# VectorE writes the low part of x from the PSUM bank in the first four groups of the first FFN

## Chip, core and metric

The kernel runs on one core of a Trainium2 chip. The metric is the device time of one launch in microseconds (us); lower is better. Engines are TensorE (PE in the profile), VectorE (DVE), ScalarE (ACT), GpSimd (POOL) and SyncE (SP), each with an instruction stream of its own that runs in order; they are kept in step by semaphores.

## What is computed

x has 32 sequences of 256 tokens with 128 features. The block is a macaron: half an FFN, attention, half an FFN, each on a layernorm of x and added to x.

```python
x = x + 0.5 * ffn(layernorm(x), router_w, w1, w2)
x = x + attn(layernorm(x), W_qkv, W_out)      # 16 heads of 8, rotary, elu+1 features, linear attention
x = x + 0.5 * ffn(layernorm(x), router_w, w1, w2)
...
probs = sigmoid(x @ router_w.T)               # 8 experts, widths 4 x 128 and 4 x 256
topw, sel = top_k(probs, 2); topw = topw / topw.sum()
h = square(relu(x @ W1[e])); y = h @ W2[e]; out = sum over e of y * combine[e]
```

The kernel computes all experts for all tokens and scales the hidden units by the square root of the routing weight before they are squared.

## The kernel before

A **group** is two sequences, 512 tokens; there are 16 (NG). Three streams run over the groups, one behind the other: `f1` (first FFN), `at` (attention) and `f2` (second FFN, SHIFT = 5 groups behind f1). Every engine runs the same loop of rounds t = -3 to 21, and the order in a round is written out by hand in its `iteration(t, par)`. In round t, f1's group t + 2 is transposed, scored by the router and has its weights broadcast; group t + 1 is in its up and down products; group t + 3 gets its layernorm statistics.

A round has 24 places (1536 hidden units are 12 chunks of 128). As long as f2 has not begun, f1 is alone (`alone`) and its 12 chunks take every second place; afterwards f1 has places 0 to 11 and f2 12 to 23.

Matmuls in fp32 precision are built from three products of high and low parts: `x_hi`, the value rounded to fp32r, and `x_lo`, what is left. The path of a group of f1 at its start:

1. `norm` (ACT, L697) writes xn; `transpose` (PE, L471) puts xn's transpose into the bank `tp`.
2. `evacuate_x` (ACT, L709) copies `tp` to `xT` in SBUF.
3. `logits` (PE, L490) multiplies xT by the router and writes the result **into tp**, over the transpose.
4. `exp_logits` (ACT, L718 ex, L722 odds), `take_sigmoid` (DVE, L972 prob), `best_two` to `choose_two` (DVE), `root_of_weights` (POOL, L874), `spread_roots` (DVE, L1025, L1031), `weight_rows` (PE, L480), `rows_of_weights` (ACT, L730), and in `broadcast` (SP) two DMAs: to DRAM (L395) and back over all partitions into `g_all` (L407, four pieces).
5. `high_part` (DVE, L965) casts xT to `x_hi` and raises s_hi; `low_part` (POOL, L868) subtracts it from xT into `x_lo` and raises s_lo. The first up product of the group waits for s_lo.
6. Per chunk: `up` (PE, L509 to L511), `weighted` (DVE, L1047, hid; the first of a group waits for the first piece of g_all), `squares` (ACT, L740 the square, L751 h_hi), `remainders` (POOL, L880, h_lo), `down` (PE, L529 to L531).

The order around the change: DVE has weighted(t, 0), then high_part of f1's group t + 2, then weighted(t, 1). PE has places 0 to 2, then logits of group t + 2, then the filler transposes `keep_busy` (L589: 36 in round -2, 16 in round -1) and place 3 on; chunk 2 is at place 4 and waits for the hid of chunk 0. ACT has exp_logits of group t + 2 ahead of the squares of places 0 to 2. POOL has low_part of group t + 2, then the h_lo of places 0 and 1, then `inv_std` (L856 ve, L857, L859 rstd, L861 nbias) of group t + 3, which waits for `mean_variance` (DVE, L957); that one stands behind place 4 and take_sigmoid. `norm` of group t + 3 waits for nbias.

```python
if c < 2:
    m = turns(s, t) * NC
    ...
m = n * NC + max(c - 1, 0)
if due(m):
    pe.wait_ge(s_z[s], value(m))
```

Of the kernel before, what the change touches and what calls it, by code (L numbers as in the profile page):

```python
# [27 lines left out]
F32 = mybir.dt.float32  # L28
F32R = mybir.dt.float32r
ALU = mybir.AluOpType  # L30
# [33 lines left out]
SHIFT = 5  # L64
T_FIRST, T_LAST = -3, NG + SHIFT

class Step:
# [14 lines left out]
    @property  # L82
    def last(self):
        return self.c + self.a * (self.trips - 1)

    @property
    def value(self):
        return self.i * self.a + self.c


def first(v):
    return v.c if isinstance(v, Step) else v
# [16 lines left out]
def live(n):  # L109

    return first(n) >= 0 and last(n) < NG


def first_time(stream, n):

    return stream and not isinstance(n, Step) and n == 0
# [51 lines left out]
def build(nc, x_in, wqkv, wout, router, w1, w2, const, out, rows):  # L168
    ctx = ExitStack()
    with ctx:  # L170
        def sb(name, shape, dt=F32):
            return ctx.enter_context(nc.sbuf_tensor(name, shape, dt))
# [35 lines left out]
        x_hi = {s: [sb(f"x_hi_{s}{u}", [P, NTOK], F32R) for u in range(nx[s])] for s in STREAMS}  # L208
        x_lo = {s: [sb(f"x_lo_{s}{u}", [P, NTOK], F32R) for u in range(nx[s])] for s in STREAMS}
# [53 lines left out]
        tp = bank[0]  # L263
# [16 lines left out]
        def per(name, keys):  # L280
            return {s: sem(f"s_{name}_{s}") for s in keys}
# [9 lines left out]
        s_hi = per("hi", STREAMS)  # L291
        s_lo = per("lo", STREAMS)
# [37 lines left out]
        def alone(s, t):  # L330


            return not live(t + 1 - SHIFT) if s == "f1" else not live(t + 2)

        def lonely(s, n):

            return n < SHIFT if s == "f1" else n >= NG - 1 - SHIFT

        def aside(s, n):

            return lonely(s, n) and ((SHIFT - n) % 2 == 1 if s == "f1" else (NG - SHIFT - n) % 2 == 0)
# [105 lines left out]
        def _(pe):  # L447
# [35 lines left out]
            def logits(s, n):  # L483
                if not live(n):
                    return
                pe.wait_ge(s_xT[s], value(n + 1))
                if first_time(s == "f1", n):
                    pe.wait_ge(s_router, 16)
                for k in range(TG):
                    i = mm(tp[:, k * P:k * P + PAD], xT[s][:, k * P:(k + 1) * P], router_sb[:], start=True, stop=True)  # L490
                i.then_inc(s_logit[s], 1)
# [150 lines left out]
            def iteration(t, par):  # L642
                transpose("f1", t + 2, t, 0)
                quarter(t, 0, par)
                state(t - 2)
                logits("f1", t + 2)
                if first_time(True, t + 2):
                    keep_busy(a2, 36)
# [15 lines left out]
                out_proj(t - 2)  # L664
                q(t - 1)
                logits("f2", t + 2 - SHIFT)
                quarter(t, 5, par)
                weight_rows("f1", t + 2, t, 4)
# [171 lines left out]
        def _(pool):  # L840
# [20 lines left out]
                gp.tensor_tensor(nbias[s][:], nm[s][:], rstd[s][:], ALU.mult).then_inc(s_nb[s], 1)  # L861

            def low_part(s, n, par):
                if not live(n):
                    return
                u = par if nx[s] == 2 else 0
                pool.wait_ge(s_hi[s], value(n + 1))
                gp.tensor_tensor(x_lo[s][u][:], xT[s][:], x_hi[s][u][:].bitcast(F32), ALU.subtract).then_inc(s_lo[s], 1)  # L868
# [14 lines left out]
            def iteration(t, par):  # L883
                remainders(t - 1, 21, 22)
                low_part("f1", t + 2, par)
                remainders(t - 1, 23)
                remainders(t, 0, 1)
                inv_std("f1", t + 3)
                remainders(t, 2, 3, 4, 5, 6)
                root_of_weights("f1", t + 2)  # L890
                remainders(t, 7)
                low_part("at", t - 1, 0)
                remainders(t, 8, 9, 10)
                low_part("f2", t + 2 - SHIFT, (par + SHIFT) % 2)
                remainders(t, 11)
                remainders(t, 12, 13, 14, 15)
                inv_std("at", t)
                remainders(t, 16, 17, 18)
                root_of_weights("f2", t + 2 - SHIFT)
                remainders(t, 19)  # L900
                inv_std("f2", t + 3 - SHIFT)
                remainders(t, 20)
                if first_time(True, t + 2):
                    pool.wait_ge(s_w2hi, 1)
                    gp.tensor_tensor(w2_lo[:], w2_raw.rearrange("p (c d) -> p c d", c=NC),
                                     w2_hi[:].bitcast(F32), ALU.subtract).then_inc(s_w2lo, 1)
# [5 lines left out]
        def _(dve):  # L912
            v = nc.vector
# [46 lines left out]
            def high_part(s, n, par):  # L960
                if not live(n):
                    return
                u = par if nx[s] == 2 else 0
                dve.wait_ge(s_xT[s], value(n + 1))
                v.tensor_copy(x_hi[s][u][:], xT[s][:]).then_inc(s_hi[s], 1)  # L965


            def take_sigmoid(s, n):
# [183 lines left out]
            def iteration(t, par):  # L1152
# [7 lines left out]
                q_features(t - 2)  # L1160
                weighted(t, 0)
                high_part("f1", n1, par)
                spread_roots("f2", n2_last, 0)
                weighted(t, 1)
# [23 lines left out]
                normalise(t - 2, 2)  # L1188
                weighted(t, 10)
                high_part("at", t - 1, 0)  # L1190
                choose_two("f1", n1)
                weighted(t, 11)
                weighted(t, 12)
                high_part("f2", n2, p2)
                spread_roots("f1", n1, 0)
                weighted(t, 13)
# [63 lines left out]
```

## Time and profile before

| what | us |
|---|---|
| median of 3 runs (lowest, highest) | 792.01 (791.9, 795.37) |
| the profiled execution | 793.06 |
| its span, first to last instruction | 791.3 |
| GpSimd busy in the span | 686.2 (87%) |
| TensorE busy | 729.2 (92%) |
| VectorE, ScalarE busy | 581.6 (74%), 597.5 (76%) |
| mean granted clock of TensorE | 0.993 |

The page gives, for each engine, its busy time, then its busy share in 40 slices, the chain of work that ended last, and the costliest groups of instructions. The timelines list single instructions with their start, their duration and, in brackets, how long the engine had been idle and who released it. The matmuls of one engine overlap, so their starts say more than their durations. A busy share is a mean over the span: the first 100 us, where the pipeline of groups fills, have other limits than the rest.

### The profile page before, as it was taken

To read this page: it belongs to the slowest core of one execution; us is meant where nothing else is said; L and a number is where in the kernel's file an instruction comes from. 1 tells how busy PE (TensorE), PEld (TensorE's weight loads), DVE (VectorE), ACT (ScalarE), POOL (GpSimd) and SP (SyncE) were. 2 spreads that over 40 slices of the span, in tenths; PEclk is the share of its full clock that TensorE was granted. 3 is DMA by queue.
4 is the path that set the end of the run, shared out by engine and by line. 5 is a ranking of instruction groups with operands and counts; after the bars stand their busy time and mean duration, and the time that the engine had idled before them with its cause. 6 is when DMAs were issued, how large, how long until landed. Compare 5 with 4: busy or idle time off the path is not lost.

```text
span 791.3 us, 13302 instructions
## 1 busy us (share of the span) xinstructions
PE 729.2 (92%) x3736; PEld 594.3 (75%) x3736; DVE 581.6 (74%) x1832; ACT 597.5 (76%) x1220; POOL 686.2 (87%) x668
## 2 busy tenths in 40 slices
PE   6688788889999999999999999999999998989887
PEld 6466566667888888888888888888887877767665
DVE  3456788877879787877878797878777678676543
ACT  4577677668887978888888879788878766766765
POOL 3778867859999999999999999999999877666876
PEclk9999999989999999999999999999999999999999
DMA  5654113023233222233333332213333403303330
GB/s 181 187 163 133 37 72 107 2 107 108 108 109 121 91 91 69 99 110 108 121 109 120 109 122 84 79 68 112 116 108 121 122 2 107 110 13 121 121 121 27
DMA packets 31160, 79.38 MB, mean 100 GB/s; under 512 B 3312, under 2 KB 14448, under 8 KB 31088
## 3 DMA queue, kind: packets, MB, share of 16 engines
q1 hardware_dynamic: 30800, 78.47, 29.9%
q8 instruction: 30, 0.49, 0.3%
q14 instruction: 42, 0.34, 0.1%
q10 hardware_dynamic: 288, 0.07, 0.0%
HBM read 73.81 MB, written 4.72 MB: 99 GB/s over the span
## 4 chain that ended last, share of the span: by engine, by line
PE 27%; DVE 27%; POOL 18%; issue 13%; ACT 10%; DMA 4%; DVEq 1%; POOLq 0%; ACTq 0%; SPq 0%
POOL h_lo L880 9%; DVE hid L1047 7%; POOL root_f L874 4%; PE bank L509 4%; PE bank L529 3%; PE bank L511 3%; PE bank L510 3%; PE bank L531 3%; PE bank L530 3%; DMA g_all_f<-rows_f 3%; ACT h_hi L751 3%; DVE pick_f L1025 2%; ACT hid L740 2%; POOL x_lo_at L868 2%; ACT xn_f L697 2%
## 5 line engine op out<-in xcount | busy, mean ns | idle before, releaser
L880 POOL TENSOR_TENSOR h_lo<-hid,h_hi 128x512 fp32r<-128x512 f32 x384 | 492.8, 1308 | 70.0 <-ACT h_hi L751 69.4
L1047 DVE SCALAR_TENSOR_TENSOR hid<-bank,g_all_f 128x512 f32<-128x512 f32 x384 | 262.2, 684 | 137.8 <-PE bank L511 90.9
L740 ACT ACTIVATE hid<-hid 128x512 f32<-128x512 f32 x384 | 228.8, 622 | 50.0 <-DVE hid L1047 49.7
L751 ACT ACTIVATE h_hi<-hid 128x512 fp32r<-128x512 f32 x384 | 225.8, 620 | 4.9 <-PE bank L531 0.4
L509 PE MATMUL bank<-x_hi_f,w_hi 128*128 128x512 f32 x384 | 164.3, 428 | 16.1 <-DVE hid L1047 16.1
L529 PE MATMUL bank<-h_hi,w_hi 128*128 128x512 f32 x384 | 154.5, 402 | 12.5 <-POOL h_lo L880 12.5
L531 PE MATMUL bank<-h_hi,w_lo 128*128 128x512 f32 x384 | 152.6, 397 | 0.0
L511 PE MATMUL bank<-x_hi_f,w_lo 128*128 128x512 f32 x384 | 151.9, 396 | 0.0
L530 PE MATMUL bank<-h_lo,w_hi 128*128 128x512 f32 x384 | 151.9, 396 | 0.0
L510 PE MATMUL bank<-x_lo_f,w_hi 128*128 128x512 f32 x384 | 151.5, 395 | 0.0
L509 PEld LDWEIGHTS bank<-x_hi_f,w_hi 128*128 128x128 f32 x384 | 73.1, 190 | 40.7 <-DVE hid L1047 25.2
L529 PEld LDWEIGHTS bank<-h_hi,w_hi 128*128 128x128 f32 x384 | 72.5, 189 | 34.9 <-POOL h_lo L880 20.0
L511 PEld LDWEIGHTS bank<-x_hi_f,w_lo 128*128 128x128 f32 x384 | 72.6, 189 | 17.6
L531 PEld LDWEIGHTS bank<-h_hi,w_lo 128*128 128x128 f32 x384 | 72.4, 188 | 16.6
L530 PEld LDWEIGHTS bank<-h_lo,w_hi 128*128 128x128 f32 x384 | 72.5, 189 | 15.4
L510 PEld LDWEIGHTS bank<-x_lo_f,w_hi 128*128 128x128 f32 x384 | 73.3, 191 | 11.1
L697 ACT ACTIVATE xn_f<-x_sb,nbias_f,rstd_f 128x128 f32<-128x128 f32 x128 | 52.4, 481 | 12.5 <-POOL nbias_f L861 12.5
L874 POOL TENSOR_TENSOR root_f<-cwt_f,c_half 128x8 f32<-128x8 f32 x32 | 54.3, 1697 | 0.0
L868 POOL TENSOR_TENSOR x_lo_f<-xT,x_hi_f 128x512 fp32r<-128x512 f32 x32 | 41.5, 1298 | 12.9 <-DVE x_hi_f L965 12.9
L709 ACT ACTIVATE xT<-bank 128x512 f32<-128x512 f32 x48 | 28.3, 590 | 26.4 <-PE bank L471 16.7
L965 DVE CAST x_hi_f<-xT 128x512 fp32r<-128x512 f32 x32 | 21.6, 676 | 24.3 <-ACT xT L709 24.3
L718 ACT ACTIVATE ex_f<-bank 128x32 f32<-128x32 f32 x32 | 6.3, 197 | 43.0 <-PE bank L490 43.0
(105 smaller groups left out, 1045.2 us busy)
## 6 DMA issues: line engine op xcount, KB each, us to landing
g_all_f<-rows_f SPq DMA_DIRECT2D x128, 512.0 KB, 5.8
x_sb<-in_x SPq DMA_DIRECT2D x16, 256.0 KB, 3.3
out_x<-x_sb SPq DMA_DIRECT2D x16, 256.0 KB, 7.1
g_all_f<-in_w SPq DMA_DIRECT2D x2, 768.0 KB, 6.6
con<-in_const SPq DMA_DIRECT2D x1, 584.0 KB, 6.1
rows_f<-g_row_f SPq DMA_DIRECT2D x32, 16.0 KB, 1.4
g_all_f<-in_wqkv SPq DMA_DIRECT2D x1, 192.0 KB, 6.5
con<-in_const ACTq DMA_DIRECT2D x1, 68.0 KB, 3.2
```

Of the source, the lines that this page charges most:

```text
L509: mm(o, w1_hi[:, w], x_hi[s][u][:], start=True, stop=False)
L510: mm(o, w1_hi[:, w], x_lo[s][u][:], start=False, stop=False)
L511: mm(o, w1_lo[:, w], x_hi[s][u][:], start=False, stop=True).then_inc(s_p1[s], 1)
L529: mm(o, w2_hi[:, c, :], h_hi[:, c, :], start=(c == 0), stop=False)
L530: mm(o, w2_hi[:, c, :], h_lo[:, c, :], start=False, stop=False)
L531: i = mm(o, w2_lo[:, c, :], h_hi[:, c, :], start=False, stop=(c == NC - 1))
L697: i = fn(xn[s][:, k, :], tile, ACT.Identity, bias=nbias[s][:, k:k + 1], scale=rstd[s][:, k:k + 1])
L740: fn(h, h, ACT.Square).then_inc(s_sq[s], 1)
L751: fn(h_hi[:, c, :], hid[:, c % STAGE, :], ACT.Copy).then_inc(s_hhi[s], 1)
L874: gp.tensor_tensor(root[s][:], cwt[s][:], c_half[:], ALU.pow).then_inc(s_root[s], 1)
L880: gp.tensor_tensor(h_lo[:, c, :], hid[:, c % STAGE, :], h_hi[:, c, :].bitcast(F32), ALU.subtract).then_inc(s_hlo[s], 1)
L1047: v.scalar_tensor_tensor(hid[:, c % STAGE, :], hp[c % 2][:], 0.0, g_all[s][:, EXPERT[c], :], ALU.max, ALU.mult).then_inc(s_z[s], 1)
```

## The change

For f1's groups 0 to 3 (`low_from_bank`), VectorE does the subtraction itself, right behind the cast: it waits for its own s_hi, reads the transpose from the bank `tp` and not from the copy xT, writes x_lo and raises s_lo. GpSimd's low_part returns at once for these groups. Since the logits overwrite `tp`, TensorE's logits of these groups wait for s_lo as well. Lines behind the first edit move down by 4 to 10.

```diff
--- before.py
+++ after.py
@@ -332,6 +332,10 @@
 
             return not live(t + 1 - SHIFT) if s == "f1" else not live(t + 2)
 
+        def low_from_bank(s, n):
+
+            return s == "f1" and n < SHIFT - 1
+
         def lonely(s, n):
 
             return n < SHIFT if s == "f1" else n >= NG - 1 - SHIFT
@@ -484,6 +488,8 @@
                 if not live(n):
                     return
                 pe.wait_ge(s_xT[s], value(n + 1))
+                if low_from_bank(s, n):
+                    pe.wait_ge(s_lo[s], value(n + 1))
                 if first_time(s == "f1", n):
                     pe.wait_ge(s_router, 16)
                 for k in range(TG):
@@ -861,7 +867,7 @@
                 gp.tensor_tensor(nbias[s][:], nm[s][:], rstd[s][:], ALU.mult).then_inc(s_nb[s], 1)
 
             def low_part(s, n, par):
-                if not live(n):
+                if not live(n) or low_from_bank(s, n):
                     return
                 u = par if nx[s] == 2 else 0
                 pool.wait_ge(s_hi[s], value(n + 1))
@@ -963,6 +969,10 @@
                 u = par if nx[s] == 2 else 0
                 dve.wait_ge(s_xT[s], value(n + 1))
                 v.tensor_copy(x_hi[s][u][:], xT[s][:]).then_inc(s_hi[s], 1)
+                if low_from_bank(s, n):
+                    dve.wait_ge(s_hi[s], value(n + 1))
+                    v.tensor_tensor(x_lo[s][u][:], tp[:], x_hi[s][u][:].bitcast(F32), ALU.subtract) \
+                        .then_inc(s_lo[s], 1)
 
 
             def take_sigmoid(s, n):
```

VectorE's order from the end of the set-up into round -2; f1's x tiles are named x_hi_f and x_lo_f, w_lo is the low part of w1. Before:

```order
L922 TENSOR_TENSOR w_lo<-g_all_f,w_hi 128x1536 [waits s_w1hi]
L965 CAST x_hi_f<-xT 128x512 [waits s_xT_f1]
L948 BN_STATS bn_f<-x_sb 128x6 [waits s_load1,s_nb_f1]
L948 BN_STATS bn_f<-x_sb 128x6 x3
L972 RECIPROCAL prob_f<-odds_f 128x32 [waits s_odds_f1]
```

After:

```order
L928 TENSOR_TENSOR w_lo<-g_all_f,w_hi 128x1536 [waits s_w1hi]
L971 CAST x_hi_f<-xT 128x512 [waits s_xT_f1]
L974 TENSOR_TENSOR x_lo_f<-bank,x_hi_f 128x512 [waits s_hi_f1]
L954 BN_STATS bn_f<-x_sb 128x6 [waits s_load1,s_nb_f1]
L954 BN_STATS bn_f<-x_sb 128x6 x3
L982 RECIPROCAL prob_f<-odds_f 128x32 [waits s_odds_f1]
```

A subtraction with the bank as its operand stands between the cast and the statistics; in each of the next three rounds it stands likewise behind the cast, which follows the first hid product:

```order
L1057 SCALAR_TENSOR_TENSOR hid<-bank,g_all_f 128x512 [waits s_p1_f1,s_ga_f10]
L971 CAST x_hi_f<-xT 128x512 [waits s_xT_f1]
L974 TENSOR_TENSOR x_lo_f<-bank,x_hi_f 128x512 [waits s_hi_f1]
L1057 SCALAR_TENSOR_TENSOR hid<-bank,g_all_f 128x512 [waits s_p1_f1]
L954 BN_STATS bn_f<-x_sb 128x6 [waits s_load0,s_nb_f1]
L954 BN_STATS bn_f<-x_sb 128x6 x3
L1057 SCALAR_TENSOR_TENSOR hid<-bank,g_all_f 128x512 [waits s_p1_f1,s_ga_f11]
```

VectorE before, at the same place in round -1:

```order
L1047 SCALAR_TENSOR_TENSOR hid<-bank,g_all_f 128x512 [waits s_p1_f1,s_ga_f10]
L965 CAST x_hi_f<-xT 128x512 [waits s_xT_f1]
L1047 SCALAR_TENSOR_TENSOR hid<-bank,g_all_f 128x512 [waits s_p1_f1]
L948 BN_STATS bn_f<-x_sb 128x6 [waits s_load0,s_nb_f1]
L948 BN_STATS bn_f<-x_sb 128x6 x3
L1047 SCALAR_TENSOR_TENSOR hid<-bank,g_all_f 128x512 [waits s_p1_f1,s_ga_f11]
```

The new row is behind the hid product that waits for the broadcast (s_ga_f10), and before the hid product of chunk 1.

TensorE in round -1, from the up product of chunk 1 over the logits and the fillers to chunk 2, before:

```order
L509 MATMUL bank<-x_hi_f,w_hi 128x512
L510 MATMUL bank<-x_lo_f,w_hi 128x512
L511 MATMUL bank<-x_hi_f,w_lo 128x512
L490 MATMUL bank<-router_sb,xT 128x96 [waits s_xT_f1]
L490 MATMUL bank<-router_sb,xT 128x96 x3
L589 MATMUL bank<-con 128x128 x16
L509 MATMUL bank<-x_hi_f,w_hi 128x512 [waits s_z_f1]
L510 MATMUL bank<-x_lo_f,w_hi 128x512
L511 MATMUL bank<-x_hi_f,w_lo 128x512
```

After:

```order
L515 MATMUL bank<-x_hi_f,w_hi 128x512
L516 MATMUL bank<-x_lo_f,w_hi 128x512
L517 MATMUL bank<-x_hi_f,w_lo 128x512
L496 MATMUL bank<-router_sb,xT 128x96 [waits s_lo_f1,s_xT_f1]
L496 MATMUL bank<-router_sb,xT 128x96 x3
L595 MATMUL bank<-con 128x128 x16
L515 MATMUL bank<-x_hi_f,w_hi 128x512 [waits s_z_f1]
L516 MATMUL bank<-x_lo_f,w_hi 128x512
L517 MATMUL bank<-x_hi_f,w_lo 128x512
```

The order is the same; the logits have s_lo_f1 as a further wait, which VectorE now raises behind its first hid product.

GpSimd's order loses the x_lo rows of groups 0 to 3 and nothing takes their place: the one of group 0 stood ahead of inv_std of group 1, the others each ahead of the h_lo of place 0 of their round.

## Rows read from the trace of the kernel before

**Rows 1.** Busy tenths of GpSimd in 40 equal slices of the span, from the page

```profile
POOL 3778867859999999999999999999999877666876
```

**Rows 2.** Waits, 0 to 170 us: waiting instruction, releaser, us in total, times, longest

```profile
DVE hid L1047 <- DMA g_all_f<-rows_f: 15.6, 3, 7.1
```

**Rows 3.** Timeline, round -2: start us, us, engine, line, instruction [idle before]

```profile
11.27 1.13 PE L490 MATMUL bank<-router_sb,xT 128*128 128x96 f32 x8 [0.69 <-ACT xT L709]
...
12.33 0.42 DVE L965 CAST x_hi_f<-xT 128x512 fp32r<-128x512 f32 x1
...
12.66 0.32 ACT L722 ACTIVATE odds_f<-ex_f,c_one 128x32 f32<-128x32 f32 x1
...
13.45 0.33 DVE L972 RECIPROCAL prob_f<-odds_f 128x32 f32<-128x32 f32 x1
...
15.81 1.63 POOL L874 TENSOR_TENSOR root_f<-cwt_f,c_half 128x8 f32<-128x8 f32 x1
```

**Rows 4.** Timeline, round -1, same columns

```profile
20.69 1.04 PE L490 MATMUL bank<-router_sb,xT 128*128 128x96 f32 x8
...
21.56 1.91 PE L589 MATMUL bank<-con 128*128 128x128 f32 x16
...
26.05 0.69 DVE L1047 SCALAR_TENSOR_TENSOR hid<-bank,g_all_f 128x512 f32<-128x512 f32 x1 [7.11 <-DMA g_all_f<-rows_f]
26.66 0.42 DVE L965 CAST x_hi_f<-xT 128x512 fp32r<-128x512 f32 x1
...
26.80 0.51 PE L509 MATMUL bank<-x_hi_f,w_hi 128*128 128x512 f32 x1 [3.33 <-DVE hid L1047]
...
27.71 0.64 ACT L740 ACTIVATE hid<-hid 128x512 f32<-128x512 f32 x1 [0.30 <-DVE hid L1047]
...
28.37 0.67 DVE L1047 SCALAR_TENSOR_TENSOR hid<-bank,g_all_f 128x512 f32<-128x512 f32 x1
28.94 1.29 POOL L880 TENSOR_TENSOR h_lo<-hid,h_hi 128x512 fp32r<-128x512 f32 x1 [0.49 <-ACT h_hi L751]
...
29.22 0.32 DVE L957 BATCH_NORM_AGGREGATE mv_f<-bn_f 128x2 f32<-128x6 f32 x4
...
30.19 0.20 POOL L856 TENSOR_TENSOR ve_f<-mv_f,c_eps 128x4 f32<-128x4 f32 x1
...
30.61 1.01 POOL L859 TENSOR_TENSOR rstd_f<-ve_f,c_mhalf 128x4 f32<-128x4 f32 x1
```

**Rows 5.** Timeline, round 0

```profile
47.67 1.03 PE L490 MATMUL bank<-router_sb,xT 128*128 128x96 f32 x8
...
49.47 0.69 DVE L1047 SCALAR_TENSOR_TENSOR hid<-bank,g_all_f 128x512 f32<-128x512 f32 x1 [4.12 <-DMA g_all_f<-rows_f]
...
52.36 1.30 POOL L880 TENSOR_TENSOR h_lo<-hid,h_hi 128x512 fp32r<-128x512 f32 x1 [0.48 <-ACT h_hi L751]
```

**Rows 6.** Timeline, round 1

```profile
72.45 1.02 PE L490 MATMUL bank<-router_sb,xT 128*128 128x96 f32 x8
...
73.64 0.69 DVE L1047 SCALAR_TENSOR_TENSOR hid<-bank,g_all_f 128x512 f32<-128x512 f32 x1 [4.38 <-DMA g_all_f<-rows_f]
...
74.25 0.66 DVE L965 CAST x_hi_f<-xT 128x512 fp32r<-128x512 f32 x1
...
76.78 1.31 POOL L880 TENSOR_TENSOR h_lo<-hid,h_hi 128x512 fp32r<-128x512 f32 x1 [0.49 <-ACT h_hi L751]
```

**Rows 7.** Groups of VectorE over the span: count | busy us, mean ns | idle before

```profile
L1055 DVE TENSOR_TENSOR x_sb<-bank,x_sb 128x512 f32<-128x512 f32 x32 | 21.7, 680 | 6.4 <-PE bank L542 6.4
```

**Rows 8.** TensorE's timeline, then busy us by stretch; granted clock third from last

```profile
88.20 0.50 PE L556 MATMUL bank<-x_hi_at,wq_hi 128*128 128x512 f32 x1 [3.47 <-POOL x_lo_at L868]
...
168.55 0.80 PE L509 MATMUL bank<-x_hi_f,w_hi 128*128 128x512 f32 x1 [2.47 <-DVE hid L1047]
...
170.00:172.00 2.00, 2.00 (x11) 2.00 (x10) 0.69 (x1) 0.00 (x0) 0.44 (x1) 0.51 0.00 0
172.00:174.00 2.00, 2.00 (x14) 1.79 (x14) 0.31 (x1) 1.01 (x4) 0.00 (x0) 1.00 0.00 0
```


## The prediction

> **What bounds the kernel now.** I read the slices of the page first. GpSimd (the page's POOL) shows 8 tenths or less in most of the first nine slices and nines only from there on [rows 1]: it bounds the steady part, not the start. The change touches groups 0 to 3 of the first FFN alone, so the question is what bounds the first 80 us. There the waits say that VectorE (DVE) stood 15.6 us in three waits for the broadcast of the routing weights [rows 2]: nobody is full, and each round is one serial loop. Its members, in the timelines: logits, ScalarE (ACT) ex and odds, VectorE's top two, GpSimd's root, the g_row copy, the two DMAs, the first hid product, its square and high part, GpSimd's first h_lo, rstd of a later group, and so on. A microsecond put on this loop has no idle time behind it that would take it back. I call the rounds t = -2 to 1; round t transposes and scores group t + 2.
>
> **What the change does to the order.** VectorE gets one instruction per round, right behind the x_hi cast. GpSimd loses one. The third edit matters most: TensorE's logits, which overwrite the bank that VectorE now reads, must also wait for x_lo. In rounds -1, 0 and 1 the x_hi cast stands behind the first hid product in VectorE's order, and that one waits for the broadcast. Today the logits are long done by then: in round -1 they start at 20.69, and x_hi only at 26.66 [rows 4]; in round 0 at 47.67 against a first hid at 49.47 [rows 5]; in round 1 at 72.45 against 73.64 [rows 6]. Afterwards they start behind hid, x_hi and x_lo. Queued behind them are, on TensorE, the filler transposes of round -1 and the up product of chunk 2, and on ScalarE ex and odds, which stand ahead of the square of chunk 0.
>
> **Price of the new subtraction.** No row has it as such. Nearest is x_sb<-bank,x_sb, a two-operand operation on 128x512 with one operand in the bank: 680 ns over 32 of them [rows 7]. The hid product, also from a bank, takes 0.69 [rows 4]. From below, the cast alone takes 0.42 and from above GpSimd's own 1.3 bounds it. I take 0.69; the lower end would take 4 x 0.27 = 1.1 us from the sum below, the upper end add 4 x 0.61 = 2.4. Waiting on the engine's own last result costs little: the cast of 12.33 ends at 12.75, and I allow 0.03 for the wait.
>
> **Round -2.** Now logits start at 11.27, x_hi at 12.33 for 0.42, odds at 12.66 for 0.32, prob at 13.45 (held back by the statistics in front of it, since odds ended at 12.98), root at 15.81 [rows 3]. Afterwards x_lo runs 12.78 to 13.47, logits start at 13.53 (+2.26), odds end at 15.24, prob starts at 15.30: **+1.85** for all that follows, root among it. GpSimd's saved 1.27 doesn't shorten this, since its next work waits for VectorE.
>
> **Round -1.** From the first hid at 26.05: x_hi 26.66 to 27.08, x_lo 27.11 to 27.80, logits at 27.86. Two branches then meet in rstd (GpSimd L859, now at 30.61) [rows 4].
> - ScalarE: from the start of the logits to the start of odds it is 1.39 (11.27 to 12.66 [rows 3]), 0.23 more to the square of chunk 0, 0.54 to that of chunk 1: 30.0. Today the latter is at 27.71 and h_lo 1.23 later, at 28.94. So h_lo would come at 31.3, +2.35.
> - TensorE: the logits take 0.96 before the next can start, 16 filler transposes 1.87 (1.91 with the last one's tail), so the up product of chunk 2 starts at 30.7 instead of 26.80. It takes 0.9, hid of chunk 2 starts at 31.6 instead of 28.37. From that start to the end of mean and variance (29.22 plus 0.32) is 1.17 today: 32.8, and rstd 0.5 later at 33.3 (ve starts 0.42 before rstd, at 30.19), **+2.7**. This one is last.
>
> **Rounds 0 and 1.** There are no fillers, only one down product (0.7) between logits and chunk 2. Round 0: hid 49.47, x_hi at 50.08, x_lo until 51.22, logits 51.28 instead of 47.67; odds 52.7, squares 52.9 and 53.5, h_lo 54.7 instead of 52.36 [rows 5]: **+2.4**. The TensorE branch gives a mean and variance at 55.7, before that h_lo ends at 56.0, so it is covered by 0.3. Round 1: x_hi takes 0.66 there [rows 6], x_lo ends at 75.63, h_lo 79.1 instead of 76.78: **+2.4**. GpSimd's three low parts of 1.3 us in these rounds lie in idle time today (it waits for h_hi behind each), so leaving them out gives nothing. VectorE's extra work of 0.69 is inside these sums.
>
> At full clock the sum is 1.85 + 2.7 + 2.4 + 2.4 = 9.35 us.
>
> **The clock.** In round -1 TensorE would stand from the end of chunk 1's up product (the logits followed it at 20.69) until 27.86, 7 us, where today the gap is 3.33 [rows 4]. The longest gap of the first 100 us, 3.47 us before 88.20, left the granted clock at 1.00; but one of 2.47 us before 168.55 is followed by a granted clock of 0.51 in the stretch 170 to 172, half speed being 1.2 of 2.4 GHz, and by 1.00 from 172; the L509 matmul that ends that gap takes 0.80 [rows 8], the one that ends the gap of 3.33 takes 0.51 [rows 4]. A gap twice the longest that was borne will, I think, cost the clock. From 168.55 to 172 the clock was low for some 3.4 us. At up to twice their time the logits (0.96) take about 1.8 and the first half of the fillers (0.93) about 1.6, which uses those 3.4 us up; the other half takes 0.93 as before: 4.3 instead of 2.8, **+1.5**. Rounds 0 and 1 have gaps of 3.6 and 3.2, like the two that kept the clock; I leave them at full speed, with up to 0.8 for the logits and 1 for the chunk-2 branch each if they don't.
> The Trainium skill, page "TensorE: Matmul & The Clock Gate", Part 1, has the rule behind this: idleness throttles the array to half clock, and activity releases it. By that rule alone each of the three rounds is at risk, and the sum could be 13; by the two gaps of rows 4 and 8 only the longest is. The same page, Part 4 (PE-mode transpose), says that transposes don't count as activity, so that the fillers would not bring the clock back; no row here decides that for fillers alone after a fall, and by it round -1 would cost about 1 us more.
>
> **Sum: 9.35 + 1.5 = 10.85 us.** The profiled execution took 793.06 (span 791.3 and 1.8 around it), 1.05 above the median of 792.01. Put on the profiled execution the sum gives 803.9, on the median 802.9. I forecast the median's.
>
> **Rivals.**
> - *Full clock everywhere*: 792.0 + 9.35 = 801.3. For it: two gaps over 3 us did no harm. Against: 7 us is another length.
> - *Half clock in two or more rounds*: 1 to 1.8 us more for each of rounds -2, 0, 1: 804 to 807. For it: the fall after 2.47 us.
> - *Part of the delay is given back*: if later rounds have slack, for example because loads of x that share the DMA engines are over by then and the broadcasts land sooner, it might be up to half: 792 + 5.4 = 797.4. Against: VectorE stood idle for the broadcasts themselves [rows 2], and no row shows other work that the start waits for.
> - *The logits' wait doesn't bind* and only the instruction put into VectorE's order counts: 4 x 0.7 = 2.8 us, 795. That needs x_lo to come before the logits would start anyway; the orders and rows 4 to 6 speak against it in three of four rounds.
> - *Faster*: GpSimd, the engine that bounds the steady part, loses 4 x 1.30 = 5.2 us: 787. It decides if GpSimd's queue, not ScalarE's h_hi, were last before each first h_lo in rounds -1 to 1. It would have to stand without a wait there, and in each of them it begins h_lo after waiting. The four low parts lie outside the slices where GpSimd is full [rows 1].
>
> **Chances.** Forecast 0.40; full clock 0.22; more half clock 0.20; part given back 0.09; insertion only 0.05; faster 0.04. The range is 798.5 to 806.5: it leaves out the last two, some of the highest, and half of the given-back case, less than 2 in 10. 0.5% (4.0 us) is about what a measurement of this kernel can tell from no change. Slower by more than that: the first four, 0.91 less a little, 0.90; within: 0.06; faster: 0.04.
>
> **What the profile after would show.** The subtraction from the bank at about 0.69; logits of rounds -1, 0 and 1 starting 1.8 to 2.1 us behind the start of the first hid, with TensorE released by VectorE's x_lo; square of chunk 0 behind odds; rstd +2.7 to +4 late in round -1; the first hid late by 1.9 in round -1, 6.1 in round 0, 8.5 in round 1 and 10.9 in round 2 (at about 96 us today), and constant from there; a granted clock under 1 near 30 us. Wrong would be: a broadcast that lands on time although g_row is late, a shift at 100 us that is not there at the end, or logits that start as early as today.

## The result and the profile after

The changed kernel takes 805.42 us in the median of 6 runs, the kernel before 791.95 of 6 on the same chip: a ratio of 1.0171, 95% interval 1.0152 to 1.019. It is slower by 13.5 us; the forecast was 10.9 slower, at 802.9, with a range of 798.5 to 806.5. The profiled execution of the changed kernel took 804.79 (span 803.0).

The page of the changed kernel: busy time by engine, granted clock of TensorE in 40 slices, and two costly groups (busy us, mean ns | idle before, releaser).

```profile
PE 734.1 (91%) x3736; PEld 600.2 (75%) x3736; DVE 584.6 (73%) x1836; ACT 597.2 (74%) x1220; POOL 681.2 (85%) x664
...
PEclk9899899999999999999999999999999999999999
...
L724 ACT ACTIVATE ex_f<-bank 128x32 f32<-128x32 f32 x32 | 6.3, 198 | 60.0 <-PE bank L496 60.0
L496 PE MATMUL bank<-router_sb,xT 128*128 128x96 f32 x256 | 36.6, 291 | 14.9 <-DVE x_lo_f L974 12.3
```

GpSimd is 5 us less busy and VectorE 3 us more, as the diff says. But TensorE now stands idle 14.9 us ahead of the logits (0.7 before), 12.3 of it for VectorE's x_lo, and ScalarE's ex waits 60.0 us for the logits (43.0 before). The clock row has two eights, in the slices that hold rounds -1 and 1. The waits of 0 to 110 us name the steps behind that (us in total, times, longest); GpSimd's wait for the first of these was 11.6 us before:

```profile
POOL h_lo L886 <- ACT h_hi L757: 25.2, 8, 7.2
ACT ex_f L724 <- PE bank L496: 21.7, 4, 7.9
...
PE bank L496 <- DVE x_lo_f L974: 12.3, 3, 5.6
```

Now the timeline, in the same columns as [rows 3 to 6]. Round -2 of the changed kernel:

```profile
13.69 1.10 PE L496 MATMUL bank<-router_sb,xT 128*128 128x96 f32 x8 [2.67 <-issue]
...
17.79 1.63 POOL L880 TENSOR_TENSOR root_f<-cwt_f,c_half 128x8 f32<-128x8 f32 x1
...
20.76 0.34 SPq L399 DMA_DIRECT2D rows_f<-g_row_f  x1
22.24 0.81 SPq L411 DMA_DIRECT2D g_all_f<-rows_f  x2
```

Root comes 1.98 later than in [rows 3]. Round -1:

```profile
26.53 0.69 DVE L1057 SCALAR_TENSOR_TENSOR hid<-bank,g_all_f 128x512 f32<-128x512 f32 x1 [5.60 <-DMA g_all_f<-rows_f]
...
27.59 0.69 DVE L974 TENSOR_TENSOR x_lo_f<-bank,x_hi_f 128x512 fp32r<-128x512 f32 x1
...
28.43 2.00 PE L496 MATMUL bank<-router_sb,xT 128*128 128x96 f32 x8 [5.59 <-DVE x_lo_f L974]
30.21 3.28 PE L595 MATMUL bank<-con 128*128 128x128 f32 x16
...
32.70 1.29 POOL L886 TENSOR_TENSOR h_lo<-hid,h_hi 128x512 fp32r<-128x512 f32 x1 [7.15 <-ACT h_hi L757]
33.25 0.48 PE L515 MATMUL bank<-x_hi_f,w_hi 128*128 128x512 f32 x1
...
35.98 1.01 POOL L865 TENSOR_TENSOR rstd_f<-ve_f,c_mhalf 128x4 f32<-128x4 f32 x1
```

The logits started ahead of the first hid product in [rows 4], at 20.69; now they start behind it and behind both halves of x, and take 2.00 instead of 1.04. The fillers take 3.28 instead of 1.91, so that the up product of chunk 2 starts 4.8 us behind the start of the logits. From the first hid to rstd it is 9.45 us where [rows 4] have 4.56. Rounds 0 and 1 have the same order, again with slow logits:

```profile
54.85 0.69 DVE L1057 SCALAR_TENSOR_TENSOR hid<-bank,g_all_f 128x512 f32<-128x512 f32 x1 [4.13 <-DMA g_all_f<-rows_f]
...
56.74 1.86 PE L496 MATMUL bank<-router_sb,xT 128*128 128x96 f32 x8 [3.54 <-DVE x_lo_f L974]
...
62.88 1.01 POOL L865 TENSOR_TENSOR rstd_f<-ve_f,c_mhalf 128x4 f32<-128x4 f32 x1
...
82.42 0.69 DVE L1057 SCALAR_TENSOR_TENSOR hid<-bank,g_all_f 128x512 f32<-128x512 f32 x1 [4.33 <-DMA g_all_f<-rows_f]
...
84.61 2.00 PE L496 MATMUL bank<-router_sb,xT 128*128 128x96 f32 x8 [3.15 <-DVE x_lo_f L974]
...
91.04 1.01 POOL L865 TENSOR_TENSOR rstd_f<-ve_f,c_mhalf 128x4 f32<-128x4 f32 x1
```

TensorE by stretch (columns: length, busy us with instructions, granted clock, DMA share, GB/s):

```profile
28.00:30.00 2.00, 1.57 (x7) 0.50 1.00 386
30.00:32.00 2.00, 2.00 (x11) 0.50 0.64 220
32.00:34.00 2.00, 2.00 (x12) 0.75 0.48 164
...
58.00:60.00 2.00, 2.00 (x7) 0.50 0.72 249
...
86.00:88.00 2.00, 2.00 (x7) 0.50 0.01 4
```

0.50 is 1.2 of 2.4 GHz. The prediction had the clock low in round -1 alone; it was low in all three. Each time the engine had stood still for the wait just before. In shorter stretches the low clock lasts from 26.2 to 33.0 us in round -1, from 56.9 in round 0 and from 84.2 in round 1.

### The profile page after: what moved, and what is told of

Read it like the earlier page. It is cut to its first block, busy times and chain, and to the rows that moved or that the text cites. A ratio compares the mean times of both kernels' runs of the same rounds, so it can differ in the third digit from the quotient of the medians.

```text
span 803.0 us, 13305 instructions
## 1 busy us (share of the span) xinstructions
PE 734.1 (91%) x3736; PEld 600.2 (75%) x3736; DVE 584.6 (73%) x1836; ACT 597.2 (74%) x1220; POOL 681.2 (85%) x664
## 4 chain that ended last, share of the span: by engine, by line
PE 30%; DVE 28%; issue 14%; POOL 12%; ACT 11%; DMA 4%; DVEq 1%; POOLq 0%; ACTq 0%; SPq 0%
DVE hid L1057 8%; POOL h_lo L886 5%; POOL root_f L880 4%; PE bank L515 4%; PE bank L517 3%; PE bank L535 3%; PE bank L516 3%; PE bank L537 3%; PE bank L536 3%; DMA g_all_f<-rows_f 3%; PE bank L496 3%; ACT h_hi L757 3%; DVE pick_f L1035 2%; ACT hid L746 2%; POOL x_lo_at L874 2%
## 5 line engine op out<-in xcount | busy, mean ns | idle before, releaser
L535 PE MATMUL bank<-h_hi,w_hi 128*128 128x512 f32 x384 | 155.2, 404 | 10.4 <-POOL h_lo L886 10.4
L517 PEld LDWEIGHTS bank<-x_hi_f,w_lo 128*128 128x128 f32 x384 | 72.9, 190 | 17.6
L703 ACT ACTIVATE xn_f<-x_sb,nbias_f,rstd_f 128x128 f32<-128x128 f32 x128 | 52.5, 481 | 11.3 <-POOL nbias_f L867 11.3
L496 PE MATMUL bank<-router_sb,xT 128*128 128x96 f32 x256 | 36.6, 291 | 14.9 <-DVE x_lo_f L974 12.3
L496 PEld LDWEIGHTS bank<-router_sb,xT 128*128 128x128 f32 x256 | 35.3, 208 | 17.8 <-issue 16.4
```

What stands on the lines that cost most here:

```text
L517: mm(o, w1_lo[:, w], x_hi[s][u][:], start=False, stop=True).then_inc(s_p1[s], 1)
L535: mm(o, w2_hi[:, c, :], h_hi[:, c, :], start=(c == 0), stop=False)
```

## The experiments

Where a round is named, "hid to rstd" is the time from the start of its first hid product to the start of rstd in that round. In the profiled kernel before it is 4.56, 4.58 and 4.83 in rounds -1, 0 and 1; in the changed kernel 9.45, 8.03 and 8.62. The difference given for a run is that of its median to the median of the kernel before on the same chip.

### Which part costs: the wait, the instruction, or the bank

**Only the wait.** This is the kernel before, with GpSimd still subtracting; TensorE's logits of groups 0 to 3 wait for x_lo:

```
@@ logits(s, n), kernel before
+                if s == "f1" and n < SHIFT - 1:
+                    pe.wait_ge(s_lo[s], value(n + 1))
```

> The kernel before, with one edit: TensorE's logits of groups 0 to 3 also wait for s_lo, which GpSimd raises as before. Theory W (the stall of the logits is the cost): x_lo comes from GpSimd some 0.2 us later than from VectorE (1.29 instead of 0.69 long, but the first work after the cast), so 805 to 807. Theory I (the instruction put into VectorE's order is the cost): no VectorE instruction is added, so 792. The square of chunk 1 may come 0.6 us earlier than in the changed kernel, but it stands behind odds, so that should not show.

809.39 against 793.03 us, ratio 1.0197 (1.0165 to 1.0228), 16.4 us slower, and above the 805 to 807 that was expected. The wait in its trace:

```profile
PE bank L492 <- POOL x_lo_f L870: 13.6, 3, 5.8
```

Hid to rstd is 10.56 in round -1 and 8.65 in round 0. The wait alone costs more than the change. GpSimd's subtraction takes 1.27 where VectorE's takes 0.69, and from the start of the cast to the logits it is 1.91 in round -1 where the changed kernel has 1.29: the logits come 0.6 later a round. The clock was low in round -2 as well, which it wasn't in the profiled changed kernel. How the 2.9 us between the two runs divide between these isn't settled.

**Only the instruction.** VectorE subtracts from xT in SBUF, so the logits need no new wait:

```
@@ VectorE, kernel before (GpSimd leaves these groups out, as in the change)
+                if low_from_bank(s, n):
+                    dve.wait_ge(s_hi[s], value(n + 1))
+                    v.tensor_tensor(x_lo[s][u][:], xT[s][:], x_hi[s][u][:].bitcast(F32), ALU.subtract) \
+                        .then_inc(s_lo[s], 1)
```

> The changed kernel without the logits' wait for s_lo; since the bank may then be overwritten, VectorE subtracts from xT in SBUF and not from the bank. Theory W: no stall, so only hid of chunk 1 comes 0.7 us later in rounds -1, 0 and 1, which shifts the square of chunk 1, h_hi and the first h_lo: 792 + 3 x 0.7 = 794, with round -2 absorbed. Theory I: the whole 13 us stays, 805.

794.41 against 793.03 us, ratio 1.0018 (1.0001 to 1.0035), 1.4 us slower. Hid to rstd is 5.29, 5.29 and 5.95: the 0.7 of the instruction each time, and about 1.1 in round 1.

**The same change, logits into another bank.** VectorE still reads the bank; only the shared bank is gone, and with it the logits' wait (the next transposes into the first bank wait for x_lo instead):

```
@@ logits(s, n) and ex, changed kernel; the fillers go to a1
-                if low_from_bank(s, n):
-                    pe.wait_ge(s_lo[s], value(n + 1))
...
-                    i = mm(tp[:, k * P:k * P + PAD], xT[s][:, k * P:(k + 1) * P], router_sb[:], start=True, stop=True)
+                    i = mm((a2 if low_from_bank(s, n) else tp)[:, k * P:k * P + PAD], xT[s][:, k * P:(k + 1) * P], router_sb[:], start=True, stop=True)
```

> The changed kernel, but the logits of groups 0 to 3 go into another bank that is free then (the fillers go to a third), so they need not wait for x_lo; VectorE still reads the transposed x from its bank and writes the low part. The wait for x_lo moves to the next writer of that bank. Theory (the shared bank's wait is what costs): logits start as early as before, in rounds -1 to 1 ahead of the first hid product, rstd minus first hid at 5.3, 5.3 and 5.9 as where VectorE subtracted without the wait; 793 to 795. Rival (reading the bank on VectorE is itself the cost): 800 or more.

794.94 against 791.97 us, ratio 1.0044 (1.0029 to 1.0059), 3.0 us slower. Its round -1:

```profile
23.13 1.85 PE L496 MATMUL bank<-router_sb,xT 128*128 128x96 f32 x8
...
25.40 0.69 DVE L1057 SCALAR_TENSOR_TENSOR hid<-bank,g_all_f 128x512 f32<-128x512 f32 x1 [5.71 <-DMA g_all_f<-rows_f]
...
30.70 1.01 POOL L865 TENSOR_TENSOR rstd_f<-ve_f,c_mhalf 128x4 f32<-128x4 f32 x1
```

The logits run ahead of hid again and hid to rstd is 5.30. (They take 1.85 because the clock was low from 18.5 to 25.3 us in this execution, behind a gap of 2.44 us; the first hid waits for the DMA anyway.) With the bank shared the change costs 13.5, with the logits elsewhere 3.0: the wait for the shared bank is shown to be the cause of some 10.5 us. The 3.0 that are left (2.3 to 4.7) fit the price of the rival "insertion only" (2.8); the run with only the instruction measured 1.4 (0.1 to 2.8).

### Which groups cost

The test in low_from_bank is narrowed to one group:

```
@@ low_from_bank(s, n), changed kernel
-            return s == "f1" and n < SHIFT - 1
+            return s == "f1" and n == 0
```

> The change for group 0 alone. In the trace of the changed kernel g_row is written 1.98 us late in round -2, but the first hid starts only 0.48 us late, since the first rows DMA took 1.5 instead of 3.2 us. Theory of the give-back by that DMA: 792.4, no difference to be measured. Theory of the prediction's sum: +1.85, 793.8. In the trace the rows DMA of round -2 is to land near 22.2 us.

Group 0 alone (round -2): 794.05 against 793.03 us, ratio 1.0012 (0.9997 to 1.0028). Its DMA of the routing rows is issued at 20.91, 2.1 later than in the kernel before, but only 1.0 of it stands in the time. The interval, -0.2 to 2.2 us, takes in no change and the forecast 1.85 alike, so the run doesn't decide between them. This trace also showed a thing that the change doesn't cause: that DMA took 3.44 us, where the changed kernel's had taken 1.48.

With `n == 1` in place of `n == 0`:

> The change for group 1 alone. Theory W with the clock: round -1 costs 4.9 us as in the trace of the changed kernel (stall of 5 to 6 us, logits and fillers at half clock), 797, and rounds 0 and 1 are as before. Theory W without the clock: 2.7 us, 794.7. If the delay of one round is given back later, under 794.

Group 1 alone (round -1): 796.41 against 793.03 us, ratio 1.0039 (1.0022 to 1.0055), 3.4 us slower. In its trace the logits wait and run slowly in round -1 alone:

```profile
24.66 0.69 DVE L1057 SCALAR_TENSOR_TENSOR hid<-bank,g_all_f 128x512 f32<-128x512 f32 x1 [5.10 <-DMA g_all_f<-rows_f]
...
26.56 1.99 PE L496 MATMUL bank<-router_sb,xT 128*128 128x96 f32 x8 [3.59 <-DVE x_lo_f L974]
...
34.96 1.01 POOL L865 TENSOR_TENSOR rstd_f<-ve_f,c_mhalf 128x4 f32<-128x4 f32 x1
```

Hid to rstd is 10.3 here, 5.7 above the kernel before, of which 3.4 reach the end (1.7 to 4.4). The DMAs of the routing rows say where most of the rest went: against the second execution of the kernel before (below) the one at 162 us is 6.6 later and the one at 186 only 5.0, which then stays until 765 us; the spans differ by 4.5. In between, the clock is low in both traces, at different places (158 to 161 and 168 to 171 us in that one, 163 to 169 in this one); whether that is the cause isn't shown.

### What the clock costs

**Fillers ahead of the wait in rounds -1 to 1.** They keep TensorE busy while it waits. No work is left out:

```
@@ TensorE's iteration(t, par), changed kernel
                 state(t - 2)
+                if not isinstance(t, Step) and -1 <= t <= 1:
+                    keep_busy(a2, 40 if t == -1 else 24)
                 logits("f1", t + 2)
```

> The changed kernel with filler transposes ahead of the logits, where TensorE stands: 40 in round -1, 24 each in rounds 0 and 1, at 0.11 us each, so that they end before x_lo is there. Theory C (half clock is worth about 4 us in rounds -1 to 1): granted clock stays at 1.00 until 90 us, first hid of rounds 0, 1 and 2 come 1.4, 2.6 and 4 us earlier than in the changed kernel, 801. If the stall alone costs and the clock does not: 805.

805.13 against 792.45 us (ratio 1.0136, 1.01 to 1.0173); one of its four runs took 799.29. In the profiled execution hid to rstd is 7.24, 7.26 and 7.26, that is 2.7, 2.7 and 2.4 above before; round 0 was still partly slow, behind a gap of 2.47 us that the 24 fillers left. So the steps from hid to rstd went as the full-clock sum says, but the time hardly moved: 805 was the number expected if the clock were worth nothing. The trace shows two other delays. Round -2 had no fillers ahead of its logits, so they ran at half clock behind a gap of 3.62 us (1.96 us long, where the changed kernel has 1.10), and the DMA of the rows was issued 0.8 late, at 21.58. And in round 0 SyncE took 4.28 us to issue the four pieces of g_all, where the changed kernel and the next run take 1.78, and the first hid came 7.22 us behind the issue of the rows instead of 5.50; nothing in the edit explains that one. Together they are 2.5 us, and the span is 2.4 longer than that of the next run (803.1 against 800.7). Round -2 shows one thing more:

```profile
15.41 4.93 PE L595 MATMUL bank<-con 128*128 128x128 f32 x36
```

```profile
14.00:16.00 2.00, 2.00 (x11) 0.50 0.00 0
...
18.00:20.00 2.00, 2.00 (x21) 1.00 0.00 0
```

From 15.41 to 20.3 TensorE runs nothing but the 36 fillers that stand behind the logits of round -2 (here the busy time is TensorE's alone), and in the midst of them, at 17.1, the clock comes back.

**Fillers in all four rounds, and more of them:**

```
+                if -2 <= t <= 1:
+                    keep_busy(a2, (20, 40, 36, 26)[t + 2])
```

> The changed kernel, with filler transposes ahead of the logits' wait in all four rounds: 20, 40, 36 and 26 of them, to keep TensorE busy up to x_lo. The work is whole otherwise. Theory (sum of full-clock terms 9.35, less 0.5 to 1 that comes back at the end): granted clock 1.00 through 10 to 90 us, rstd minus first hid +2.7, +2.4, +2.4 against before, the first out_x some 9.3 later, 799.5 to 801.5. Rival (the clock falls elsewhere whatever is filled, or fillers delay what stands behind them): 803 to 806.

801.32 against 791.97 us, ratio 1.0115 (1.0099 to 1.0131), 9.35 us slower (7.8 to 10.4), which is the full-clock sum of the prediction. That it agrees to the digit is partly chance, as the rows DMAs below show. Round -1 in its trace, then TensorE by stretch:

```profile
26.44 0.69 DVE L1059 SCALAR_TENSOR_TENSOR hid<-bank,g_all_f 128x512 f32<-128x512 f32 x1 [5.58 <-DMA g_all_f<-rows_f]
...
28.55 1.03 PE L496 MATMUL bank<-router_sb,xT 128*128 128x96 f32 x8
29.42 1.91 PE L595 MATMUL bank<-con 128*128 128x128 f32 x16
...
33.83 1.01 POOL L867 TENSOR_TENSOR rstd_f<-ve_f,c_mhalf 128x4 f32<-128x4 f32 x1
```

```profile
24.00:26.00 2.00, 2.00 (x18) 0.92 1.00 268
26.00:28.00 2.00, 2.00 (x20) 1.00 1.02 358
28.00:30.00 2.00, 2.00 (x21) 1.00 0.98 376
```

Everything between hid and rstd stands near where the prediction put it: 7.39 us, 2.8 above before. In rounds 0 and 1 it is 7.60 and 7.40 (3.0 and 2.6 above; the fillers themselves held the logits up by some 0.2 in round -1 and 0.4 in round 0). The clock wasn't at 1.00 throughout, as had been expected: it was low from 21 to 24.3, where the first hid waits for the DMA anyway, and again from 96. Against the second execution of the kernel before, the rows DMA of round 2 is 10.5 us later, that of round 3 11.3, and from 190 us on it is 9.35. So the four rounds cost somewhat more than the sum, and 1.9 came back.

The same waits, then, cost 9.35 us with the clock kept behind them and 13.5 without: **the clock is worth some 4.1 us** (both intervals together leave about 2 us either way; at the rows DMA of round 2 the two traces differ by 3.8). The forecast had 1.5 for it; the 2.6 between them are as large as its whole miss.

**Without the 16 fillers of round -1** (the last call of keep_busy left out of the changed kernel):

```
-                if first_time(True, t + 1):
-                    keep_busy(a2, 16)
```

> The changed kernel without the 16 filler transposes behind the logits of round -1. Theory of the TensorE branch (fillers, then chunk 2, then mean and variance are last in round -1): chunk 2 comes 2 to 3 us earlier and rstd is then bound by h_lo at about 34.4 instead of 35.98, 804. If the fillers matter for the clock, it stays at half for longer and most of the gain is lost: 805.

803.39 against 792.45 us, ratio 1.0133 (1.0104 to 1.0161), 10.9 us slower and so 2.5 better than the changed kernel, though the two intervals overlap. Hid to rstd of round -1 is 7.86 instead of 9.45. The fillers stand in front of the up product of chunk 2, as the prediction said, and cost there 1.6 us, at a clock that is half for nearly all of them.

**The kernel before once more**, unchanged, to see what varies by itself:

> The kernel before, unchanged, in a second profiled execution: what differs between it and the first is what one execution differs from another. 792 us. Asked of it: the first DMA of the routing rows (3.19 us in the first execution, 1.48 in the changed kernel's, 3.44 in that of group 0 alone). If this varies by itself, it will be 1.5 or 3.2 to 3.5 here; and whether the granted clock keeps 1.00 from 10 to 100 us.

792.34 us (span 790.6). In the first execution the DMA of the rows and the one behind it, which waits for it, were issued at

```profile
18.78 0.34 SPq L395 DMA_DIRECT2D rows_f<-g_row_f  x1
21.97 1.29 SPq L407 DMA_DIRECT2D g_all_f<-rows_f  x3
```

and in this one, with its first hid, the q matmul and a stretch of TensorE:

```profile
18.88 0.34 SPq L395 DMA_DIRECT2D rows_f<-g_row_f  x1
20.37 2.35 SPq L407 DMA_DIRECT2D g_all_f<-rows_f  x4
...
24.71 0.69 DVE L1047 SCALAR_TENSOR_TENSOR hid<-bank,g_all_f 128x512 f32<-128x512 f32 x1 [5.65 <-DMA g_all_f<-rows_f]
...
86.66 0.80 PE L556 MATMUL bank<-x_hi_at,wq_hi 128*128 128x512 f32 x1 [3.46 <-POOL x_lo_at L868]
```

```profile
86.00:88.00 2.00, 1.34 (x3) 0.55 0.00 0
```

Two things differ from [rows 4] and [rows 8] with no edit at all. The DMA of the rows takes 1.49 instead of 3.19, and the first hid comes 1.34 earlier. And the same q matmul, behind the same 3.46 us of idleness, finds the clock at half (0.80 us) where in the first execution it found it full (0.50, at 88.20). The row that the prediction took as proof that a gap of 3.5 us is borne was one of two outcomes, and the rarer one: the q matmul stands behind 3.46 or 3.47 us of idleness in 12 of the 14 traces, and the clock fell in 11 of them. Nor does the duration of that matmul tell. In the run with the early cast and groups 2 and 3 (below) it takes 0.50 and the clock falls 1.1 us later:

```profile
87.04 0.50 PE L562 MATMUL bank<-x_hi_at,wq_hi 128*128 128x512 f32 x1 [3.47 <-POOL x_lo_at L874]
```

```profile
88.00:90.00 2.00, 2.00 (x7) 0.53 0.04 8
```

### Is it the place of the cast

**The change with the x_hi cast moved ahead of the first hid product**, so that x_lo needn't stand behind the broadcast:

```
@@ VectorE's iteration(t, par), changed kernel
+                if n1 < SHIFT - 1:
+                    high_part("f1", n1, par)
                 weighted(t, 0)
-                high_part("f1", n1, par)
+                if n1 >= SHIFT - 1:
+                    high_part("f1", n1, par)
```

> The changed kernel with the x_hi cast and the subtraction of groups 0 to 3 ahead of the first hid product in VectorE's order, so that they run while VectorE stands for the broadcast. Theory W: x_lo comes about 1.2 us after xT in rounds -1 to 1, before or about when the logits would start in the kernel before; the stall is gone, and hid of chunk 1 comes 0.4 us sooner: 791 to 793. Theory I (the work on VectorE itself): 795 or more.

796.44 against 792.45 us, ratio 1.0042 (1.0027 to 1.0057), 4.0 us slower, where 791 to 793 was expected. In rounds 0 and 1 it does what was meant: x_lo ends before the logits could start, and hid to rstd of round 0 is 4.25, shorter than before. In round -1 it doesn't:

```profile
22.27 3.43 POOL L911 TENSOR_TENSOR w_lo<-g_all_f,w_hi 128x1536 fp32r<-128x1536 f32 x1 [2.93 <-ACT w_hi L831]
...
22.70 3.29 DVE L971 CAST x_hi_f<-xT 128x512 fp32r<-128x512 f32 x1 [1.85 <-ACT xT L715]
26.02 0.69 DVE L974 TENSOR_TENSOR x_lo_f<-bank,x_hi_f 128x512 fp32r<-128x512 f32 x1
...
26.86 2.00 PE L496 MATMUL bank<-router_sb,xT 128*128 128x96 f32 x8 [3.88 <-DVE x_lo_f L974]
```

The cast takes 3.29 us instead of 0.42. It starts while GpSimd's subtraction of 3.43 us runs and ends within 0.3 us of its end (25.99 against 25.70). The Trainium skill, page "SBUF — State Buffer", section "Who interferes with whom", says that the two engines share one pair of ports as an exclusive lock, held for a whole instruction, and that casts are among the operations that can take it: this row agrees. So group 1 still waits, 3.9 us, and finds half clock, and hid to rstd of round -1 is 7.76, 3.2 above before.

**The kernel before with the same early cast**, GpSimd subtracting:

> The kernel before with the x_hi cast of groups 0 to 3 ahead of the first hid product. Hid of chunk 1 comes 0.4 us sooner in rounds -1, 0, 1, and with it its square and the first h_lo: 790.8 if that passes through, 792 if not.

790.98 against 792.45 us, ratio 0.9981 (0.9967 to 0.9996), 1.5 us faster. Hid to rstd is 4.23, 4.24 and 4.55, some 0.3 less in each round. Here too the cast of round -1 was held (3.30 us), but nothing waits for it.

**The early cast, and VectorE's low part in groups 2 and 3 alone:**

```
-            return s == "f1" and n < SHIFT - 1
+            return s == "f1" and 2 <= n < SHIFT - 1
```

> The kernel before with the x_hi cast ahead of the first hid product in groups 0 to 3, and VectorE's low part from the bank in groups 2 and 3 alone (rounds 0 and 1), the logits of these two waiting for it. There x_lo ended before the logits could start anyway in the run with the early cast in all four groups, so the wait costs nothing. Theory (the cost of the change is the place of x_hi and x_lo behind the broadcast, together with the wait; who subtracts is without weight): rstd minus first hid stays at 4.2 to 4.6 in all three rounds, 790.5 to 792 us, that is the time of the early cast alone. Rival (VectorE's own extra instruction costs its 0.7 a round): 792 to 793.5. Rival (GpSimd's saved 1.3 us per group is worth something): 789 or less.

792.36 against 791.97 us, ratio 1.0006 (0.9993 to 1.0019): no change. In rounds 0 and 1 hid to rstd is 4.23 and 4.26, and the logits stand behind x_lo without a loss (x_lo 46.83 to 47.52, logits 47.67). So where x_lo is ready in time, the change costs nothing and brings nothing. The time lies just above the expected 790.5 to 792. That the early cast alone came out 1.5 us better than before and this one not may be the scatter of the clock or the extra instruction; the two weren't run on one chip, and it stays open. No version beat the kernel before by an amount worth having.

## Why the prediction came out as it did

The time lies in the stated range, but not because the forecast's own case came true. The wait was right, and one term of the sum, the clock, was too small.

**The mechanism: right.** The logits wait for VectorE's x_lo in rounds -1, 0 and 1, and start 1.9, 1.9 and 2.2 us behind the start of the first hid (forecast 1.8 to 2.1). The wait is the cause: alone it costs 16.4 us, and with another bank 3.0 are left.

**The price of the subtraction: right.** 692 ns over the four, taken as 0.69 from the hid product and [rows 7].

**Round -2, +1.85: right within what can be told, though the two profiles first hid it.** The changed kernel's first hid is only 0.48 later than in [rows 4], because the rows DMA took 1.48 us there and 3.19 in the first execution of the kernel before. Against the second execution, whose DMA took 1.49, it is 26.53 against 24.71, or 1.82 later. With group 0 alone only 1.0 us was seen at the end, so how much of this term reaches the end by itself isn't certain to the last microsecond. The term also took the clock as full. It was in the profiled changed kernel, but not in four other runs with VectorE's low part in group 0 (group 0 alone, fillers in rounds -1 to 1, early cast, no 16 fillers): there it was low from about 14 to 17 or 18 us, and the rows DMA was issued at 20.91 to 21.58 instead of 20.76.

**Rounds -1, 0, 1 at full clock, +2.7, +2.4, +2.4: right.** With fillers they measure 2.8, 3.0 and 2.6, less the 0.2 and 0.4 that the fillers cost in rounds -1 and 0. The kernel as a whole is 9.35 us slower, as summed, but that needed 1.9 us to come back later, which the sum didn't have.

**The clock, +1.5: the step that failed.** It measures some 4.1 us (805.42 less 801.32, each against nearly the same median of the kernel before). Against the full-clock terms the changed kernel's rounds are 2.2, 1.05 and 1.4 longer (9.45, 8.03 and 8.62 less 4.56, 4.58 and 4.83, less 2.7, 2.4 and 2.4), 4.6 in the profiled pair. Two errors stand in that step. The first is in rounds 0 and 1, which were left at full speed because two gaps of the trace, 3.33 and 3.47 us, had borne it. The gaps came as forecast (3.54 and 3.15), and the clock fell; it cost 1.05 and 1.4, within the 1 to 1.8 a round that the rival had given it. The other traces show why that argument was weak. In the first 200 us of all 14 there are 32 gaps of 2.8 us or more ahead of a TensorE instruction (past the first 5 us). Behind 30 of them the clock fell, between 2.3 us before their end and 1.3 after it. The two that were borne are the two that the prediction read, both in one trace: that was bad luck. At the place of the gap of 3.33, the run of group 0 alone has one of 3.49 and a low clock. The second error is in round -1: the low clock was given 3.4 us from one example, [rows 8], but from the start of the logits it lasted 4.6, until 33.0, so that nearly all of the 16 fillers ran at half speed (3.28 together), and the round lost 2.2 and not 1.5. The rival "half clock in two or more rounds", 804 to 807, with a chance of 0.20, is what happened; the prediction's own figure for a fall in all three rounds, 13, was nearest. The rival had the fall behind 2.47 us in [rows 8] on its side, which should have weighed as much as the two gaps that were borne.

**That fillers would not bring the clock back: wrong.** In round -1 of the changed kernel the low clock did last through nearly all of the fillers, until 33.0, and without the fillers it was 0.60 in 30 to 32 and 1.00 in 32 to 34, a little earlier. But in the run with fillers in rounds -1 to 1 TensorE ran nothing but fillers from 15.41 to 20.3 and the clock rose from 0.50 to 1.00 at 17.1, and in the runs of group 0 alone and without the 16 fillers it rose at the same place, at 17.6 and 18.0. They keep it too: in the run with fillers in all rounds, nothing but such transposes ran from 24.1 until the logits at 28.55, and the granted clock was 0.92, 1.00 and 1.00 there. The Trainium skill, page "TensorE: Matmul & The Clock Gate", Part 4 (PE-mode transpose), says that a transpose doesn't count as a busy engine in the same way; these traces disagree, both for raising the clock and for keeping it.

**Nothing given back: right in the main.** Against the second execution of before, the rows DMAs of the changed kernel are later by 1.9, 6.7, 10.3 and 14.3 us in rounds -2 to 1, and from 195 us by a steady 13.5, the difference of the medians. So 0.8 came back between 170 and 195 us; with fillers in all rounds it was 1.9, and with group 1 alone 1.6. The forecast's "6.1 in round 0, 8.5 in round 1" were 6.9 and 10.8 in that comparison. At the very end the two profiled executions differ by 12.4 (spans 803.0 and 790.6); the last 1 us goes behind 738 us (the shift is 12.8 at 760) and is not explained.

**Faster, by GpSimd's 5.2 us: no sign.** GpSimd has 5 us less to do and waits 25.2 us for h_hi in the first 110 us, 11.6 before. In the run of groups 2 and 3, where nothing else is lost, its saved 2.6 us brought nothing.

## What to carry to other kernels

A read of a shared bank moved to another engine also moves the release of that bank. Ask who writes the bank next and where the new reader stands in its engine's order: here the subtraction cost 0.7 us a round and the wait of the next writer some 10 us in all. A stall of TensorE at a place where the loop is serial is paid twice, once as idleness and once as half clock on what follows; give the second a price at every such stall, also where one trace shows a gap like it that was borne. Fillers ahead of the wait bought that second part back here, some 4 of the 13.5 us. And before a row of one execution is taken for a rule, look at the same row in a second execution of the same kernel.

## What the runs showed of the hardware that was not expected

- The granted clock after the same gap is not the same from one execution to the next. Before the q matmul, 3.47 us of idleness left it at 1.00 in one trace, and 3.46 or 3.47 took it to half in 11 others. Before the up product that stands at 168.55 in [rows 8], 2.47 and 2.48 us took it to half in the two executions of the kernel before, and 2.47 left it at 1.00 in the run with fillers in all rounds.
- The fall can come ahead of the end of the gap or behind it: 1.4 us ahead of the q matmul with group 1 alone, 1.3 us behind its start without the 16 fillers, where the matmul itself still takes 0.50 us. So a fast first matmul doesn't show that a gap was borne; the granted clock of the next stretches does.
- Identity transposes with nothing else on TensorE bring a halved clock back and keep it (15.41 to 20.3 us with fillers in rounds -1 to 1, 24.5 to 28.55 with fillers in all).
- A cast on VectorE that takes 0.42 us takes 3.29 to 3.31 when it starts beside a GpSimd subtraction of 3.43 to 3.46 us (three kernels with the early cast).
- The first DMA of the routing rows takes 1.5 or 3.2 to 3.6 us in different executions, in the same kernel too, and shifts the first hid product by about as much.
